# Between the two layers: which products stand ahead of the recurrence, and where z of chunks 1 to 3 is made

## The chip, the cores and the metric

The kernel runs as one program on one core of a Trainium2 chip. The metric is the device time of one execution in microseconds (us). The core has a matrix engine (TensorE, in the profile PE, its weight loads PEld) and three engines for elementwise work: VectorE (DVE), ScalarE (ACT) and GpSimd (POOL). Each takes its own instructions in the order in which they are written and waits on semaphores for the others. SyncE (SP) issues the DMAs here. Operands lie in SBUF; matmuls write PSUM, eight banks of 128 partitions by 512 float32.

## The reference, cut to what matters

Two layers on x of 2048 tokens by 128 features. Layer 0 is an RWKV-like attention with a recurrence and a dense FFN, then a switch FFN with 8 experts. Layer 1 begins with a Mamba block and ends with 16 experts and a shared one. The change lies at the start of the Mamba block:

```python
xz = einsum('bld,ed->ble', x, in_proj_w)            # x here: layernorm(x) * (1 + ca) + sa
xb, zb = xz[..., :256], xz[..., 256:]
u  = silu(causal_conv4(xb) + conv_b)
proj = einsum('bld,ed->ble', u, x_proj_w)           # dt_raw 8, b 16, c 16, a_gate_raw 256
dt = softplus(dt_raw @ dt_proj_w.T + dt_proj_b)
a  = -exp(A_log) * (0.5 + sigmoid(a_gate_raw))
state = exp(dt * a) * state + dt * b_t * u_t        # for 256 channels x 16 states, over 2048 tokens
y_t   = sum(state * c_t) + D_param * u_t
y = y * silu(zb)                                    # zb is first needed here
out = einsum('ble,de->bld', y, out_proj_w)
```

## The kernel before, in words

Features lie on the 128 partitions and tokens along the free axis. The 2048 tokens are cut into four chunks of 512 (`NCH`, index i), the 256 inner channels into two halves (`DI`, index c). Every instruction of this part therefore has the form 128 x 512.

The order on each engine is written out by hand. `sequences()` lists the steps of each engine in order, and each step adds one to its engine's semaphore; `upto(step, i)` is the value that a waiting engine needs. Nothing is reordered at run time: what stands behind a waiting instruction waits too.

**The section between the layers.** For each chunk: the layernorm of layer 1 (`centre_e`, `var_e` on PE, `stats_e` on ACT, `norm_e` on DVE) gives HC; `xb(i)` multiplies HC by the first half of in_proj, `xb_copy` takes it to SBUF, and `conv(c, i)` on DVE adds the taps in PSUM (one scaling, three multiply-adds); `u(i)` on ACT applies Silu. `bc(i)` on PE makes b, c and dt_raw from u; `proj_out(i)` on ACT takes out b, c as bfloat16 (`bc_hi`) and dt_raw (`dt_raw_copy`). `bc_r1` (DVE), `bc_mid` (ACT) and `bc_lo` (POOL) split the rest of b and c into two further bfloat16 parts. `dt(i)` multiplies dt_raw, `softplus(i)` makes the step sizes. `z(i)` multiplies HC by the second half of in_proj and `z_silu(i)` applies Silu to it; that is silu(zb), which `gated(i)` on POOL first needs when a chunk's recurrence is over. `gate0` and `gate1` make a_gate_raw; only chunk 0 has its gates here.

PSUM is shared out by hand: chunk i has the banks i and 4+i (`half(0, i)` and `half(1, i)`), used one after the other by xb, z, bc, the gates and dt. So z(i) waits for u(i), and bc(i) waits for z_silu(i), since they use the same banks.

**The recurrence.** It is 64 turns, q = 16 i + n, for chunk i and state n. PE broadcasts b and c of the state to 128 partitions (`b{n}`, `c{n}`, banks 4 and 5). DVE multiplies b by dt u for both halves (`dbu`, one instruction of 128 x 1024), and runs two scans over the tokens (`st{n}_0`, `st{n}_1`). ACT copies c (`c_copy`) and makes the two decays with Exp (`dec`) in banks 6 and 7. POOL multiplies state by c for each half (`times_c`, `sc{n}_c`), and every second turn copies the last columns for the next chunk (`carry`); this comes behind the step of its turn in `STEP_POOL`. PE adds the products of turn q - 4 (`y_sum`). DVE issues dbu(q+1) ahead of the scans of turn q. The rings couple the engines: the scans of an even turn q wait for the carry of turn q - 3, those of an odd turn for the carry of turn q - 4.

Other work is laid into the turns by tables: `GATE_PE` and `GATE_ACT` (the gates of chunks 1 to 3: products into banks 2 and 3, a Tanh, and an Identity that adds two), `STEP_POOL` (`dtg` and `du`, one POOL multiply each), `SPLIT_AT` (every fourth turn from 18 to 50 ACT rounds and POOL subtracts a block of expert weights, `w_hi`, `w_lo`), `SIDE` (behind a chunk: skip, gated, m_out, x_mamba, the layernorm with `norm_f`, the router) and `GATE_AT` (the router's top-8, small DVE instructions, from turn 34 on). After turn 63 come 68 turns of the experts, on which the change does nothing.

**Lines.** Front: L730 xb and z; L762 bc and gates; L775 dt; L1098 u; L1103 z_silu; L1092 and L1093 proj_out; L1107 bc_mid; L1119 softplus; L1138 and L1145 table loads; L1462 and L1467 conv; L1456 bc_r1; L1268 the last step of norm_e; L1500 dtg of chunk 0; L1662 bc_lo. Recurrence: L908 b and c; L1511 dbu; L1534 scans; L1178 c_copy; L1184 dec; L1111 and L1114 the gates' Tanh and Identity; L1626 every POOL multiply (times_c, dtg, du, gated); L1700 w_lo; L815 y_sum; L1237 skip; L1516 x_mamba; L1520 and L1522 norm_f; L1548 the first step on the router's scores.

Of the kernel before, what the change touches and what calls it, by code (L numbers as in the profile page):

```python
# [58 lines left out]
def side_names(engine, k, i):  # L59
# [11 lines left out]
GATE_PE = {0: [("gate0", 1)], 1: [("gate1", 1)], 2: [("gate0", 2)], 3: [("gate1", 2)],  # L71
           4: [("gate0a", 3)], 5: [("gate0", 3)], 6: [("gate1a", 3)], 7: [("gate1", 3)]}
GATE_ACT = {1: (0, 1), 2: (1, 1), 3: (0, 2), 4: (1, 2), 6: (0, 3), 8: (1, 3)}
STEP_POOL = {4: ("dtg_0", 1), 6: ("dtg_1", 1), 8: ("du_0", 1), 10: ("du_1", 1), 12: ("dtg_0", 2), 14: ("dtg_1", 2), 16: ("du_0", 2), 20: ("du_1", 2),
             24: ("dtg_0", 3), 28: ("dtg_1", 3), 32: ("du_0", 3), 36: ("du_1", 3)}
# [3 lines left out]
       "c0", "c1", "eps5", "eps6", "two",  # L79
# [44 lines left out]
def one(*steps):  # L124
    return [(s, 0) for s in steps]


def sequences():
# [60 lines left out]
    for e in range(E0):  # L189
# [27 lines left out]
    for q in range(NQ + TURNS + LAG_E):  # L217
# [68 lines left out]
def build(nc, X_in, vec_in, core_in, cst_in, wA_in, wmod_in, cstB_in, wB1_in, wB2_in, wC_in, sel_in, eyeb_in, wD_in, out):  # L286
# [17 lines left out]
    with ctx:  # L304
# [142 lines left out]
        HC = area(te_at + T, T)  # L447
# [17 lines left out]
        DRAW = area(place_at[0] + T, T)  # L465
# [73 lines left out]
        def _(pe):  # L539
# [225 lines left out]
            def bc(i):  # L765
                pe.wait_ge(*upto("z0_silu", i))
                x_proj(half(1, i, BC3 + DTR), i, DI * P, BC3 + DTR).then_inc(*done("bc", i))

            def dt(i):
                a = wc_at["dtp"][0]  # L770
                pe.wait_ge(*upto("dt_raw_copy", i))
                for c, w in enumerate((["z1_silu"], ["bc_r1"]) if i else (["gate0_tanh"], ["gate1_tanh"])):
# [8 lines left out]
            z(1)  # L781
# [3 lines left out]
            bc(1)  # L785
            dt(0)
            z(2)
            dt(1)
            bc(2)
            z(3)  # L790
            dt(2)
            bc(3)
            dt(3)

            def gates(q):
                for step, i in GATE_PE.get(q, ()):
                    c = int(step[4])
                    cs = range(DI) if i < NCH - 1 else range(1) if step[-1] == "a" else range(1, DI)
# [124 lines left out]
        def _(act):  # L923
# [196 lines left out]

            xb_copy(2)
# [24 lines left out]
            bc_mid(3)  # L1146
# [673 lines left out]
```

## Time and profile before

| what | us |
|---|---|
| median of 3 runs | 746.44 (746.33 to 746.46) |
| the profiled execution's own time | 746.32 |
| its span, first to last instruction | 744.5 |
| busy: PE / DVE / ACT / POOL | 599.6 / 559.7 / 377.4 / 376.8 |
| mean granted clock of TensorE | 0.912 |
| first scan of the recurrence starts | 324.30 |
| the two scans of the last turn, 63, start | 564.84 |

Times in the profile count from the first instruction. Idle time of an engine costs something only where the chain of waits passes through it. A Matmul in float32 appears as two records. Positions in the recurrence are named by turn: turn q begins where its first scan begins.

### The profile page before, as it was taken

The numbers are of one execution on the slowest core, as the hardware profiler recorded it, in microseconds if no ns is written. First come the engines' busy times: TensorE is split into PE (matmuls) and PEld (weight loads), VectorE is DVE, ScalarE is ACT, GpSimd is POOL, SyncE is SP. The second block draws the span as 40 slices with busy tenths as digits, with TensorE's granted clock in tenths as the row PEclk, the third lists the DMA queues.
The fourth block names the chain that finished last, engine by engine and source line by source line (L and its number), as shares of the span: only waits on it lengthen the run. The fifth ranks groups of instructions, "written<-read, shape, count | busy, mean of one in ns | idle before, by whom it ended". The sixth has DMA issues, their size and how long they took to land.

```text
span 744.5 us, 6787 instructions
## 1 busy us (share of the span) xinstructions
PE 599.6 (81%) x1964; PEld 326.5 (44%) x1964; DVE 559.7 (75%) x771; ACT 377.4 (51%) x657; POOL 376.8 (51%) x330
## 2 busy tenths in 40 slices
PE   6696777589699977878866776677678998999997
PEld 3232222156567732223322232233224666777775
DVE  1757995735767675479999999999996775756564
ACT  4573001696554166677565663456554446544443
POOL 0005666252000110248998986779776544655554
PEclk9698766689799999989999998799999999999999
DMA  8000002400000000100001000000000000000000
GB/s 295 2 2 0 0 1 92 209 1 0 0 1 1 1 0 0 43 0 0 0 5 36 24 22 22 21 11 0 1 0 0 1 1 14 2 0 15 1 15 15
DMA packets 4036, 15.93 MB, mean 21 GB/s; under 512 B 704, under 2 KB 960, under 8 KB 3520
## 3 DMA queue, kind: packets, MB, share of 16 engines
q1 hardware_dynamic: 4000, 15.51, 5.9%
q8 instruction: 16, 0.26, 0.1%
q14 instruction: 20, 0.16, 0.1%
HBM read 14.46 MB, written 1.05 MB: 21 GB/s over the span
## 4 chain that ended last, share of the span: by engine, by line
PE 28%; POOL 22%; DVE 22%; issue 20%; ACT 6%; DMA 1%; POOLq 0%; DVEq 0%; SPq 0%; ACTq 0%
POOL h_parts L1731 11%; POOL arena L1626 10%; DVE arena L1534 9%; PE ps L547 5%; DVE arena L1511 5%; PE ps L815 2%; PE ps L762 2%; PE ps L713 2%; PE ps L675 2%; PE ps L730 1%; PE ps L698 1%; DVE arena L1325 1%; PE ps L615 1%; PE ps L684 1%; PE ps L865 1%
## 5 line engine op out<-in xcount | busy, mean ns | idle before, releaser
L1626 POOL TENSOR_TENSOR arena<-arena 128x512 f32<-128x512 f32 x186 | 229.3, 1257 | 79.8 <-DVE arena L1534 41.2
L1534 DVE TENSOR_TENSOR_SCAN arena<-ps,carry,arena 128x512 f32<-128x512 f32 x128 | 156.3, 1261 | 0.0
L1184 ACT ACTIVATE ps<-arena,abase 128x512 f32<-128x512 f32 x128 | 88.1, 691 | 98.8 <-DVE arena L1534 98.6
L815 PE MATMUL ps<-arena,core 128*128 128x512 f32 x256 | 128.4, 625 | 0.0
L1731 POOL TENSOR_TENSOR h_parts<-arena,h_parts 128x512 fp32r<-128x512 f32 x68 | 88.1, 1297 | 78.8 <-ACT h_parts L1215 78.8
L865 PE MATMUL ps<-x_parts,w_hi 128*128 128x512 f32 x272 | 99.4, 405 | 5.5 <-DVE arena L1615 2.6
L908 PE MATMUL ps<-bc,sel 96*128 96x512 bf16 x128 | 44.3, 406 | 65.4 <-DVE arena L1511 50.5
L1615 DVE TENSOR_TENSOR arena<-ps,arena 128x512 f32<-128x512 f32 x68 | 47.0, 691 | 60.9 <-PE ps L865 52.9
L1223 ACT ACTIVATE arena<-ps 128x512 f32<-128x512 f32 x68 | 40.6, 597 | 88.8 <-PE ps L865 88.8
L1511 DVE TENSOR_TENSOR arena<-ps,arena 128x1024 f32<-128x1024 f32 x64 | 76.7, 1198 | 4.2 <-PE ps L908 4.1
L815 PEld LDWEIGHTS ps<-arena,core 128*128 128x128 f32 x256 | 51.4, 201 | 39.1 <-issue 32.1
L865 PE MATMUL ps<-h_parts,w_hi 128*128 128x512 f32 x136 | 65.8, 486 | 1.2 <-POOL h_parts L1731 1.2
L908 PEld LDWEIGHTS ps<-bc,sel 96*128 96x128 bf16 x128 | 11.5, 99 | 120.1 <-DVE arena L1511 88.4
L865 PEld LDWEIGHTS ps<-x_parts,w_hi 128*128 128x128 f32 x272 | 51.3, 189 | 18.9 <-DVE arena L1615 3.0
L547 PE MATMUL ps<-arena 128*128 128x512 f32 (+2 forms) x80 | 43.3, 692 | 14.1 <-POOL arena L1626 8.5
L865 PE MATMUL ps<-x_parts,wD 128*128 128x512 f32 x136 | 53.7, 395 | 0.0
L929 ACT ACTIVATE arena<-ps 128x512 f32<-128x512 f32 x16 | 9.4, 597 | 79.8 <-PE ps L547 64.1
L1658 POOL TENSOR_TENSOR x<-arena,x 128x512 f32<-128x512 f32 x4 | 5.4, 1342 | 86.9 <-DVE arena L1449 86.9
L1619 DVE TENSOR_TENSOR arena<-ps,arena 128x512 f32<-128x512 f32 x64 | 44.3, 692 | 2.2
L1215 ACT ACTIVATE h_parts<-arena 128x512 fp32r<-128x512 f32 x68 | 42.4, 623 | 0.8 <-DVE arena L1619 0.5
L590 PE MATMUL ps<-v_parts,spread_r 128*128 128x512 f32 x64 | 29.0, 565 | 16.4 <-DVE arena L1325 14.2
L1325 DVE TENSOR_TENSOR_SCAN arena<-arena,ps 128x512 f32<-128x512 f32 x32 | 40.5, 1267 | 0.0
(223 smaller groups left out, 1008.5 us busy)
## 6 DMA issues: line engine op xcount, KB each, us to landing
arena<-in_wB SPq DMA_DIRECT2D x2, 2048.0 KB, 12.6
arena<-in_wD SPq DMA_DIRECT2D x8, 384.0 KB, 3.1
arena<-in_cstB SPq DMA_DIRECT2D x1, 1368.0 KB, 5.9
x<-in_x SPq DMA_DIRECT2D x4, 256.0 KB, 4.9
out_x<-x SPq DMA_DIRECT2D x4, 256.0 KB, 2.0
arena<-in_wA SPq DMA_DIRECT2D x1, 928.0 KB, 9.7
wC<-in_wC SPq DMA_DIRECT2D x1, 912.0 KB, 10.9
arena<-in_wmod SPq DMA_DIRECT2D x1, 768.0 KB, 6.5
```

The lines of the kernel that those rows point to most:

```text
L547: mm(half(h, i, rows), lhsT, ch(rhs, i)[0:parts], start=True, stop=True).then_inc(*done(step, i))
L815: mm(bank(c + 2 * (i % 2)), CORE_("eye"), PRC[:, (2 * q + c) % PR_RING, :], start=(n == 0), stop=(n == NS - 1)).then_inc(*done(f"y{n}_{c}" ...
L865: r = mm(out, w_parts[wp][:, k, :], x[xp], start=start and (wp, xp) == (0, 0), stop=stop and last)
L908: mm(bank(b), sel[:, row, :], BC[:, i * N:(i + 1) * N], start=True, stop=True).then_inc(*done(f"{kind}{n}", i))
L1184: A(bank(6 + c), ch(DTG[:, c, :], i), ACT.Exp, scale=ABASE[:, c * NS + n:c * NS + n + 1]).then_inc(*done(f"dec{n}_{c}", i))
L1325: nc.vector.tensor_tensor_scan(S[:, v, i * N + 1:(i + 1) * N + 1], ch(DEC, i), bank(4 + q % 4), S[:, v, i * N:i * N + 1], ALU.mult, ALU.ad ...
L1511: tt(DBU[:, a:a + DI, :], bank(4).unsqueeze(1).to_broadcast([P, DI, N]), DU[:, :, i * N:(i + 1) * N], ALU.mult).then_inc(*done(f"dbu{n}", i))
L1534: nc.vector.tensor_tensor_scan(ST[:, k % ST_RING, :], bank(6 + c), DBU[:, (2 * q + c) % DBU_RING, :], CARRY[:, k:k + 1], ALU.mult, ALU.add ...
L1615: tt(HH[:, k, :], bank(6), SG[:, k, :], ALU.mult).then_inc(*done(f"hh{e}", i))
L1619: tt(HW[:, k, :], bank(7), HH[:, k, :], ALU.mult).then_inc(*done(f"hw{e}", i))
L1626: mul = lambda o, a, b: nc.gpsimd.tensor_tensor(o, a, b, ALU.mult)
L1731: nc.gpsimd.tensor_tensor(HWP[:, 1, q % 4, :], (HW if e < E1 else HH)[:, q % 2, :], HWP[:, 0, q % 4, :].bitcast(f32), ALU.subtract).then_i ...
```

## The change

- In the section between the layers `z` and `z_silu` are left for chunk 0 alone. `xb(3)` goes ahead of `z(0)`. The order on PE becomes xb 3, z 0, bc 0, gate0, bc 1, gate1, bc 2, dt 0, bc 3, dt 1, dt 2, dt 3; ACT and DVE follow (conv(1, 2) ahead of the first bc_r1, the bc_mid further back). `bc(i)` waits for `u1` in place of `z0_silu`.
- z of chunks 1 to 3 is made in turns 10 to 15 of the recurrence: one product of PE per turn into bank 2 or 3, and on ACT, one turn later, three instructions: tanh(z/2) to ZT, z/2 to Z, and ZT + 1. POOL multiplies the two (`z_full`), six multiplies in turns 12, 14, 15, 16, 25 and 28. The other POOL steps move back by up to eight turns.
- The gates of chunks 1 to 3 start one turn later; gate1 of chunk 2 is split into two half products as those of chunk 3 are.
- HC, the tanh values and dt_raw move to other places in SBUF.

```diff
-GATE_PE = {0: [("gate0", 1)], 1: [("gate1", 1)], 2: [("gate0", 2)], 3: [("gate1", 2)],
-           4: [("gate0a", 3)], 5: [("gate0", 3)], 6: [("gate1a", 3)], 7: [("gate1", 3)]}
-GATE_ACT = {1: (0, 1), 2: (1, 1), 3: (0, 2), 4: (1, 2), 6: (0, 3), 8: (1, 3)}
-STEP_POOL = {4: ("dtg_0", 1), 6: ("dtg_1", 1), 8: ("du_0", 1), 10: ("du_1", 1), 12: ("dtg_0", 2), 14: ("dtg_1", 2), 16: ("du_0", 2), 20: ("du_1", 2),
-             24: ("dtg_0", 3), 28: ("dtg_1", 3), 32: ("du_0", 3), 36: ("du_1", 3)}
+GATE_PE = {1: [("gate0", 1)], 2: [("gate1", 1)], 3: [("gate0", 2)], 4: [("gate1a", 2)], 5: [("gate1", 2)],
+           6: [("gate0a", 3)], 7: [("gate0", 3)], 8: [("gate1a", 3)], 9: [("gate1", 3)],
+           10: [("z0", 2)], 11: [("z1", 2)], 12: [("z0", 3)], 13: [("z1", 3)], 14: [("z0", 1)], 15: [("z1", 1)]}
+GATE_ACT = {2: ("gate", 0, 1), 3: ("gate", 1, 1), 4: ("gate", 0, 2), 6: ("gate", 1, 2), 8: ("gate", 0, 3), 10: ("gate", 1, 3),
+            11: ("z", 0, 2), 12: ("z", 1, 2), 13: ("z", 0, 3), 14: ("z", 1, 3), 15: ("z", 0, 1), 16: ("z", 1, 1)}
+STEP_POOL = {4: ("dtg_0", 1), 6: ("dtg_1", 1), 8: ("du_0", 1), 10: ("du_1", 1), 12: ("z0_full", 2), 14: ("z1_full", 2), 15: ("z0_full", 3), 16: ("z1_full", 3),
+             17: ("dtg_0", 2), 20: ("dtg_1", 2), 21: ("du_0", 2), 24: ("du_1", 2), 25: ("z0_full", 1), 28: ("z1_full", 1),
+             29: ("dtg_0", 3), 32: ("dtg_1", 3), 36: ("du_0", 3), 40: ("du_1", 3)}
...
             def bc(i):
-                pe.wait_ge(*upto("z0_silu", i))
+                pe.wait_ge(*upto("u1", i))
+                if i == 0:
+                    pe.wait_ge(*upto("z0_silu", i))
...
             def gates(q):
                 for step, i in GATE_PE.get(q, ()):
+                    if step[0] == "z":
+                        c = int(step[1])
+                        pe.wait_ge(*upto(f"gate{c}_tanh", NCH - 1))
+                        if i != 2:
+                            pe.wait_ge(*upto(f"z{c}_half", {3: 2, 1: 3}[i]))
+                        a = wc_at["in"][0] + DI * P
+                        mm(bank(2 + c), wC[:, a + c * P:a + (c + 1) * P], ch(HC, i), start=True, stop=True).then_inc(*done(step, i))
+                        continue
...
+            def z_parts(c, i):
+                act.wait_ge(*upto(f"z{c}", i))
+                A(ZT[c, i], bank(2 + c), ACT.Tanh, scale=0.5).then_inc(*done(f"z{c}_tanh", i))
+                A(ch(Z[:, c, :], i), bank(2 + c), ACT.Copy, scale=0.5).then_inc(*done(f"z{c}_half", i))
+                act.wait_ge(*upto(f"z{c}_tanh", i))
+                A(ZT[c, i], ZT[c, i], ACT.Identity, bias=col("one")).then_inc(*done(f"z{c}_one", i))
...
             xb_copy(2)
             u(0)
             xb_copy(3)
             z_silu(0)
             proj_out(0)
+            u(1)
             gate_tanh(0, 0)
-            u(1)
-            bc_mid(0)
-            z_silu(1)
-            gate_tanh(1, 0)
             proj_out(1)
             u(2)
-            z_silu(2)
-            bc_mid(1)
+            gate_tanh(1, 0)
             proj_out(2)
             u(3)
-            z_silu(3)
+            bc_mid(0)
             nc.scalar.preload_act_table_set("softplus")
             softplus(0)
+            proj_out(3)
+            bc_mid(1)
+            softplus(1)
             bc_mid(2)
-            proj_out(3)
-            softplus(1)
+            bc_mid(3)
             softplus(2)
             softplus(3)
             nc.scalar.preload_act_table_set("exp_and_others")
-            bc_mid(3)
...
+            def z_full(c, i):
+                pool.wait_ge(*upto(f"z{c}_one", i))
+                mul(ch(Z[:, c, :], i), ch(Z[:, c, :], i), ZT[c, i]).then_inc(*done(f"z{c}_full", i))
```

## Rows read from the trace of the kernel before

**Rows 1.** Busy time by stretch: us, then each engine, granted clock, DMA, GB/s

```profile
281.00:324.30 43.30, 35.80 (x71) 13.05 (x72) 21.31 (x28) 27.47 (x46) 7.02 (x6) 0.88 0.06 19
...
360.00:380.00 20.00, 13.52 (x35) 5.28 (x34) 20.00 (x18) 11.02 (x18) 18.06 (x17) 1.00 0.00 0
```

**Rows 2.** Chain of waits, 304 to 326: start us, us, what

```profile
305.91 3.34 PE ps L730 x4
...
314.62 3.58 ACT arena L1119 x6
...
319.28 3.41 PE ps L762 x4
```

**Rows 3.** Timeline before turn 0: start, us, engine line, xcount, [idle before <-who ended it]

```profile
277.88 0.55 DVE L1268 TENSOR_SCALAR arena<-arena,mod 128x512 f32<-128x512 f32 x1
280.18 1.09 ACT L1098 ACTIVATE arena<-ps 128x512 f32<-128x512 f32 x2
281.43 4.58 DVE L1467 SCALAR_TENSOR_TENSOR ps<-arena,vec,ps 128x512 f32<-128x512 f32 x6
288.01 0.59 ACT L1092 ACTIVATE bc<-ps 96x512 bf16<-96x512 f32 x1 [1.57 <-PE ps L762]
290.87 1.98 PE L730 MATMUL ps<-arena,wC 128*128 128x512 f32 x4 [1.18 <-ACT arena L1098]
309.91 1.28 ACT L1138 ACT_TABLE_LOAD   x1
318.89 1.22 DVE L1511 TENSOR_TENSOR arena<-ps,arena 128x1024 f32<-128x1024 f32 x1 [1.10 <-PE ps L908]
323.16 1.22 DVE L1511 TENSOR_TENSOR arena<-ps,arena 128x1024 f32<-128x1024 f32 x1 [3.04 <-PE ps L908]
324.30 2.45 DVE L1534 TENSOR_TENSOR_SCAN arena<-ps,carry,arena 128x512 f32<-128x512 f32 x2
```

**Rows 4.** Timeline of turns 3 and 4, PE and ACT

```profile
333.34 0.60 PE L908 MATMUL ps<-bc,sel 96*128 96x512 bf16 x2
335.14 0.72 ACT L1114 ACTIVATE arena<-arena,vec 128x512 f32<-128x512 f32 x1
335.50 1.02 PE L762 MATMUL ps<-arena,wC 128*128 128x512 f32 x2
336.35 0.60 PE L908 MATMUL ps<-bc,sel 96*128 96x512 bf16 x2
```

**Rows 5.** Groups of POOL, 326 to 563: busy us, mean ns

```profile
L1626 POOL TENSOR_TENSOR arena<-arena 128x512 f32<-128x512 f32 x142 | 176.5, 1272 | 42.3 <-DVE arena L1534 40.3 <-ACT arena L1178 1.0 <-PE ps L908 0.9
L1700 POOL TENSOR_TENSOR wD<-arena,w_hi 128x768 fp32r<-128x768 f32 x8 | 14.5, 1812 | 1.8 <-ACT w_hi L1189 1.7
```

**Rows 6.** Timeline of turns 12, 28 and 34, DVE, then POOL

```profile
366.24 2.44 DVE L1534 TENSOR_TENSOR_SCAN arena<-ps,carry,arena 128x512 f32<-128x512 f32 x2
...
423.91 2.44 DVE L1534 TENSOR_TENSOR_SCAN arena<-ps,carry,arena 128x512 f32<-128x512 f32 x2
427.02 1.02 DVE L1522 TENSOR_SCALAR arena<-arena,mod 128x512 f32<-128x512 f32 x1
429.10 2.44 DVE L1534 TENSOR_TENSOR_SCAN arena<-ps,carry,arena 128x512 f32<-128x512 f32 x2
446.50 2.44 DVE L1534 TENSOR_TENSOR_SCAN arena<-ps,carry,arena 128x512 f32<-128x512 f32 x2
449.08 3.47 DVE L1548 TENSOR_SCALAR arena<-arena 128x64 f32<-128x64 f32 x1
454.13 2.45 DVE L1534 TENSOR_TENSOR_SCAN arena<-ps,carry,arena 128x512 f32<-128x512 f32 x2
...
425.26 3.91 POOL L1626 TENSOR_TENSOR arena<-arena 128x512 f32<-128x512 f32 x3
448.25 1.80 POOL L1700 TENSOR_TENSOR wD<-arena,w_hi 128x768 fp32r<-128x768 f32 x1
450.02 2.47 POOL L1626 TENSOR_TENSOR arena<-arena 128x512 f32<-128x512 f32 x2
```

More of the change, by code:

```diff
@@ L78 @@
 VEC = ["ln1_w", "mu_r", "mu_k", "mu_v", "mu_w", "mu_g", "w0", "u", "gn_w", "gn_b", "ln2_w",
-       "c0", "c1", "eps5", "eps6", "two",
+       "c0", "c1", "eps5", "eps6", "two", "one",
        "dt_b0", "dt_b1", "D0", "D1", "cb0", "cb1"] + [f"cw{c}_{j}" for c in range(DI) for j in range(KC)] + \
@@ L446, in build @@
         TE = area(te_at, T)
[L447 removed]
+        HC = over_arena("layer_in", WD_AT + 2 * T, T, f32)
+        tanh_at = [te_at + (2 + c) * N for c in range(DI)] + [WD_AT + E0 * 2 * P + k * N for k in range(4)]
+        assert tanh_at[-1] + N <= WD_AT + 2 * T
+        ZT = {(c, i): over_arena(f"z_tanh{c}_{i}", tanh_at[2 * (i - 1) + c], N, f32) for i in range(1, NCH) for c in range(DI)}
         XBP = area(xbp_at, DI * (T + 3)).rearrange("p (c t) -> p c t", c=DI)
@@ L771, in dt @@
                 pe.wait_ge(*upto("dt_raw_copy", i))
-                for c, w in enumerate((["z1_silu"], ["bc_r1"]) if i else (["gate0_tanh"], ["gate1_tanh"])):
+                for c, w in enumerate(([], ["bc_r1"]) if i else (["gate0_tanh"], ["gate1_tanh"])):
                     for name in w:
@@ L784, in _ @@
             x_proj(half(1, 0), 0, P, P).then_inc(*done("gate1", 0))
-            bc(1)
+            bc(2)
             dt(0)
-            z(2)
+            bc(3)
             dt(1)
-            bc(2)
-            z(3)
             dt(2)
-            bc(3)
             dt(3)
+            halves = [item for items in GATE_PE.values() for item in items if item[0][-1] == "a"]
             def gates(q):
                 for step, i in GATE_PE.get(q, ()):
+                    if step[0] == "z":
[6 more added lines that the diff above has]
+                        continue
                     c = int(step[4])
-                    cs = range(DI) if i < NCH - 1 else range(1) if step[-1] == "a" else range(1, DI)
+                    split = (f"gate{c}a", i) in halves
+                    cs = range(DI) if not split else range(1) if step[-1] == "a" else range(1, DI)
                     if 0 in cs and i > 1:
@@ L1486, in _ @@
             conv(0, 2)
+            conv(1, 2)
             bc_r1(0)
-            conv(1, 2)
-            bc_r1(1)
             conv(0, 3)
@@ L1495, in _ @@
             nc.vector.memset(CARRY[:], 0.0).then_inc(*done("st_zero"))
+            bc_r1(1)
             bc_r1(2)
@@ L1749 @@
     vecs = dict(L0, u=L0["u"].reshape(-1), gn_w=by_value(L0["gn_w"].reshape(-1), 0), gn_b=by_value(L0["gn_b"].reshape(-1), 0),
-                c0=a["L0_c"][0], c1=a["L1_c"][0], eps5=np.full(P, 1e-5, np.float32), eps6=np.full(P, 1e-6, np.float32), two=np.full(P, 2, np.float32))
+                c0=a["L0_c"][0], c1=a["L1_c"][0], eps5=np.full(P, 1e-5, np.float32), eps6=np.full(P, 1e-6, np.float32), two=np.full(P, 2, np.float32), one=np.full(P, 1, np.float32))
     x = np.ascontiguousarray(L0["x"][0].T)
```

40 lines of the change are left out of this document (22 added, 18 removed).

## Prediction

> **What bounds the kernel now.** I read the busy time by stretch first. Between the layers, 281 to 324.3, no engine is full: PE 35.8 of 43.3 us, ACT 27.5, DVE 21.3, and the granted clock is 0.88 [rows 1]. That is a stretch of waits. In the recurrence DVE is busy 20.00 of 20 us, PE, ACT and POOL 13.5, 11.0 and 18.1 [rows 1]: there DVE sets the pace, and POOL is the next by far.
>
> The chain of waits says which waits end last in the first stretch: the product z(3) (3.34 us, at the lower clock), the softplus run on ACT, and, behind the start of the recurrence, a gate product of 3.41 us [rows 2]. z of chunks 1 to 3 is in that chain although nobody needs it before a chunk's recurrence is over. The timeline gives the start of the recurrence [rows 3]: the last softplus ends at 318.20 (314.62 + 3.58 [rows 2]), dbu(0) starts at 318.89, dbu(1) only at 323.16, after 3.04 us without work on DVE, and the first scan at 324.30. From there DVE runs on to the experts, so what moves the first scan moves the end, if the turns keep their length.
>
> **The section between the layers.** It loses three z (six products) and six Silu, and with them the waits of bc(i) for z_silu. I follow the new order with the durations of [rows 3]: a product over both halves 1.91 apart from the next (four records, 1.98), a pair of u or z_silu 1.09, proj_out 2 x 0.62, a table 1.28, a conv of three 2.3 (4.58 for six) and 0.85 more where its scaling is on DVE; softplus 0.60 each (3.58 / 6 [rows 2]).
> - xb(3) need not wait for u(0) any more: modE(3) ends at 278.43 (277.88 + 0.55), the product at 280.4. u(0) ends at 281.27 as before, xb_copy(3) at 282.9, z(0) on PE at 282.7, z_silu(0) at 284.0, its first half at 283.5.
> - bc(0) 283.55 to 285.5, gate0 to 287.3; ACT proj_out(0) to 286.8, u(1) to 287.9; bc(1) to 289.85.
> - ACT Tanh, proj_out(1) to 291.1, u(2) to 292.2 (its conv runs through, from 286.01 = 281.43 + 4.58 to 289.15); bc(2) to 294.2, dt(0) to 296.1.
> - Conv of chunk 3 ends at 295.15 on DVE (bc_r1(0) 0.7, then 2.3 and 3.15). ACT: proj_out(2) to 295.4, u(3) to 296.55, bc_mid(0) to 297.15, table to 298.4, softplus(0) to 299.65, proj_out(3) to 300.9 (bc(3) 296.6 to 298.5).
> - From here ACT has work without a gap: bc_mid(1), softplus(1), bc_mid(2) and (3), softplus(2) and (3): 3 x 0.62 + 6 x 0.60 = 5.5, to 306.4. PE has dt(1), dt(2), dt(3) done at 300.4, 302.3, 304.3, ahead of need.
>
> So the last softplus ends at 306.4, before 318.2: **11.8 us**. ACT's removed Silus are only 3.3 of it; the rest are waits.
>
> **The start of the recurrence.** With no gate in turn 0, b(1) goes out when dbu(0) has ended. dbu(0) starts 0.65 behind the softplus (0.69 before), takes 1.22, b(1) about 0.5, dbu(1) 1.14 until the scan: 3.6 us, before 324.30 - 318.20 = 6.1. ACT covers it: table 1.28, c_copy 0.5, first decay 0.7 are over after 2.5. **2.5 us**. First scan at 310.0; 14.3 us in sum. POOL's du(0) waits only for bc_mid(0) and softplus(0) and is over by 302. If the clock is at 1.2 GHz in the three dt products, each takes up to 3.34 in place of 1.98 and ACT would wait some 3 us; if the reordered waits are all free, ACT's idle 4 us are the floor. I keep 11 to 16 for this part.
>
> **PE and ACT in the turns.** PE with a half gate takes 3.01 us from b to b (333.34 to 336.35) of a turn of 3.48; a z product takes the same 1.02 as a half gate [rows 4], in turns 10 to 15, so it hides. ACT is busy 11.02 of 20 us without gates, 1.92 a turn [rows 1]; z adds three instructions of at most 0.72 [rows 4], 1.8 to 2.2: 3.7 to 4.1, or about 3.5 when each begins some 0.1 before the last one's record ends (the records overlap so). A turn is 3.48. The decay ends about 0.9 us ahead of its scan, which covers six turns of a slip of 0.1; at 0.6 a turn the six would cost 2.7. I take zero, of 0 to 2.7. The gates one turn later cost nothing, since dtg(1) on POOL stays in turn 4. The expert weights' first DMAs hang on the last conv on SP's queue and go out 8 us earlier, into a stretch whose other work needs no DMA; the later ones wait for w_lo, up to 3 us late, for a split four turns (14 us) on: nothing.
>
> **POOL.** Six multiplies of 1.24 us (pitch; 1272 ns mean duration [rows 5]) are new: 7.4 us. A turn of POOL is 2.49 and 0.14 for a carry every second turn; it can start its first multiply 1.35 behind the first scan (425.26 - 423.91 [rows 6]), so a turn leaves it 0.9 idle; a step costs 1.24 and a split 1.77, more than the idle time. From turn 12 to turn 28 DVE needs 423.91 - 366.24 = 57.7 us [rows 6]. POOL's work in these 16 turns: 39.8 for the states, 1.1 carries, 5.3 for the splits of 18, 22 and 26, 2.5 gated of turn 21, and nine steps, before five: 11.2, before 6.2. In sum 59.9, and about 2 of waits at the start. It ends turn 27 at 61.9 of the new time, where turn 28's first multiply could start at 59.0: **2.9 us behind**. In before it is not behind there (it starts at exactly 1.35). By the same count it ends turn 34 at 88.2 where 84.1 would be on time, 4.1 behind; the most is 4.8 in turn 22.
>
> Being behind is free while the waits allow it. The scans of turn 30 need the carry of 27 (61.9 against 66.3), those of 34 that of 31 (76.4 against 80.25); PE adds the products only four turns later, so it bears some 7 us. So no scan waits for POOL.
>
> What is not free are DVE instructions that both read and write SBUF. modF of turn 28 lasts 1.02 and had begun while POOL multiplied; the router's first, 128 x 64 only, lasts 3.47 [rows 6]: it begins at 449.08, and ends at 452.55, just when POOL's run (w_lo to 450.05, two multiplies to 452.49) is over. DVE got in between two POOL instructions in the first case (427.75), and at the end of the run in the second. So:
> - low end: DVE gets in at the next boundary in turn 28 (62.0, +0.2 against before), and waits for the run's end in turn 34: 88.5 (88.2 and the 0.3 that POOL lost to modF), that is 8.1 behind the turn's begin, where before it was 6.05 (452.55 - 446.50). **2.3 us lost.** The wait lets POOL catch up, so it is paid once; turns 36 and 40 have one step each as 32 and 36 had, with POOL on time.
> - high end: it waits for the run's end in turn 28 too, to 65.9 in place of 61.8: 4.1; then turn 34 costs 0.5 more than before: **4.6 us lost**.
> - below: in turn 34 it gets in early, and 2 of the 3.4 us that before loses come back.
> I take 2.3, as each of the two waits goes as it did before.
>
> The Trainium skill (SBUF — State Buffer, Who interferes with whom) says that a DVE instruction in a two-port mode, or with two SBUF inputs, and a GpSimd instruction exclude each other, and that the second to issue is blocked until the first finishes. By this rule the cost is one POOL instruction at most, and the change would be better by 4 us than my sum; the 3.47 us, across three POOL instructions, disagree.
>
> **Sum.** 746.32 - 14.3 + 2.3 = 734.3 for an execution like the profiled one; the median is 0.12 above it. I predict **734.4**.
>
> **Rivals.**
> - *POOL is paid for in full.* Each of DVE's SBUF instructions waits for the run's end, or scans wait for the carry: 4.6 to 7.4 in place of 2.3. For: POOL 18.06 of 20 us, the 3.47. Against: the low end of the count above. 737 to 739.5; I give 738.
> - *One POOL instruction at most*, the page's rule, worked out here: in turn 34 the request at 83.0 meets the multiply that ends at 84.1, so the router's first step is over 2.3 us earlier against the turn than before, and +0.2 remains in turn 28. 746.4 - 14.3 - 2.1 = 730. For: 427.75. Against: 449.08.
> - *The front gives less.* Another wait is last, such as conv of chunk 3 or dt at 1.2 GHz; the last softplus at 311: 739.
> - *Slower.* PE falls to 1.2 GHz in turns 4 to 15: its turn of 3.01 becomes 6, as z(3) took 3.34 where z(1) took 1.98 [rows 2, 3]. Each such turn costs 2.5, and from the sixth on (2.5 x 6 > 14.3) the kernel is slower; 12 turns give 762. For: 0.88 ahead of the recurrence. Against: PE has more to do in these turns than before, and the clock was 1.00 in the later stretch with less work [rows 1].
> - That the change does not do what it says (some z back in the chain) I count with the third.
>
> **Chances.** Forecast 0.60, POOL in full 0.15, one instruction 0.12, front less 0.09, slower 0.03; 0.01 for no change. Within 0.2% (1.5 us) is what a measurement of this kernel can't tell from none. The forecast's own range is 732.5 to 736.5; with the first and second rival I give 730 to 739, which leaves the rest out. Faster 0.96, same 0.01, slower 0.03.
>
> **What would show it.** First scan near 310 and last softplus near 306.4; no DVE gap between dbu(0) and dbu(1) beyond b(1)'s 0.6; turns of 3.48 up to 19; POOL without idle time from 14 to 34; modF of turn 28 1.0 to 1.3 us (4 or more: the high end); the router's first step of turn 34 about 5.5 us. A turn above 4 between 1 and 19 would prove me wrong on PE or ACT, an idle DVE ahead of a scan on POOL's carry. The stretch from the last scan to the end should stay as it is.

## The result, and the profile after

| what | before | changed |
|---|---|---|
| median of four runs, us | 746.45 (746.33 to 754.95) | 736.14 (736.06 to 736.99) |
| ratio of the means, 95% interval | | 0.9838 (0.9802 to 0.9874) |
| the profiled execution's own time / span | 746.32 / 744.5 | 736.99 / 735.0 |
| mean granted clock | 0.912 | 0.913 |

The kernel became 10.3 us faster; 734.4 was forecast, with 730 to 739 as the range. The ratio of the medians is 0.986; that of the means is lower because one run of before took 754.95. In the later batches of this study before has medians of 746.65, 748.39, 748.33 and 748.94, and the changed kernel, run again beside the second of them, 736.44; the ratio given with each run below is against before in its own batch. Both profiled executions fall into the same pieces:

| stretch, us | before | changed | difference | forecast |
|---|---|---|---|---|
| start to the last layernorm step's end | 278.43 | 279.41 | +1.0 | 0 |
| to the end of the last softplus | 39.77 | 27.58 | -12.2 | -11.8 |
| to the first scan | 6.11 | 3.77 | -2.3 | -2.5 |
| turns 0 to 19 | 69.78 | 70.57 | +0.8 | 0 |
| turns 20 to 27 | 29.82 | 29.82 | 0 | 0 |
| turns 28 to 33 | 22.60 | 22.37 | -0.2 | +0.2 |
| turns 34 to 38 | 29.17 | 30.76 | +1.6 | +2.1 |
| turns 39 to 62 | 89.17 | 88.52 | -0.7 | 0 |
| end of the last scan (turn 63) to the end | 177.26 | 179.73 | +2.5 | 0 |

Turn 63's two scans, 2.43 us in both, lie between the last two rows. The first piece is not touched by the change: over the profiles of this study its last step starts between 276.8 and 279.7. The rest I take from the rows that follow.

The timeline before turn 0 in the changed kernel (start, us, engine and line; it answers to [rows 3]):

```profile
278.86 0.55 DVE L1289 TENSOR_SCALAR layer_in<-layer_in,mod 128x512 f32<-128x512 f32 x1
...
304.60 2.39 ACT L1135 ACTIVATE arena<-ps,vec 128x512 f32<-128x512 f32 x4
...
307.69 1.23 DVE L1532 TENSOR_TENSOR arena<-ps,arena 128x1024 f32<-128x1024 f32 x1 [4.66 <-PE ps L924]
...
309.62 1.22 DVE L1532 TENSOR_TENSOR arena<-ps,arena 128x1024 f32<-128x1024 f32 x1 [0.70 <-PE ps L924]
...
309.80 3.62 PE L768 MATMUL ps<-arena,wC 128*128 128x512 f32 x4
...
310.76 2.45 DVE L1555 TENSOR_TENSOR_SCAN arena<-ps,carry,arena 128x512 f32<-128x512 f32 x2
...
313.21 1.06 PE L924 MATMUL ps<-bc,sel 96*128 96x512 bf16 x2
...
313.88 1.22 DVE L1532 TENSOR_TENSOR arena<-ps,arena 128x1024 f32<-128x1024 f32 x1 [0.68 <-PE ps L924]
315.03 2.45 DVE L1555 TENSOR_TENSOR_SCAN arena<-ps,carry,arena 128x512 f32<-128x512 f32 x2
```

The last softplus ends at 306.99, where before it ended at 318.20; DVE now waits 0.70 us for b(1), before 3.04. But the gate product, 3.62 us long, now stands ahead of b(2): b(2) and c(2) run from 313.21 to 314.27, dbu(2) can start only at 313.88 with b(2) done, DVE waits 0.68, and turn 0 is 4.27 us (310.76 to 315.03) in place of 3.48.

The chain of waits of the same stretch (start, us, what; it answers to [rows 2]):

```profile
298.08 1.28 ACT L1157
...
299.38 1.26 ACT arena L1135 x2
300.64 0.48 ACT bc L1108
...
303.67 1.03 ACT bc L1123 x2
304.70 2.30 ACT arena L1135 x4
```

From the table load at 298.08 to the end at 306.99 ACT is busy 8.82 of 8.91 us: what ends last here is ACT's own work and no longer a product of PE. The windows, as [rows 1], with the expert stretch of both kernels and 8 us out of it (before's at 620, the changed kernel's at 608, each 55 us behind turn 63):

```profile
281.96:310.76 28.80, 24.27 (x50) 8.33 (x51) 19.13 (x28) 23.64 (x40) 8.49 (x6) 0.88 0.09 28
346.52:366.52 20.00, 17.32 (x44) 6.74 (x45) 20.00 (x19) 18.95 (x35) 18.07 (x18) 1.00 0.00 0
552.79:732.00 179.21, 173.89 (x717) 123.80 (x717) 109.91 (x215) 84.42 (x148) 97.13 (x77) 0.97 0.02 5
608.00:616.00 8.00, 5.42 (x22) 3.87 (x21) 3.81 (x6) 4.17 (x7) 2.85 (x2) 0.79 0.00 0
```

Before:

```profile
564.84:742.00 177.16, 171.38 (x717) 122.33 (x717) 110.34 (x215) 84.42 (x148) 97.10 (x77) 0.99 0.02 5
620.00:628.00 8.00, 5.94 (x29) 4.37 (x30) 5.17 (x8) 4.64 (x10) 3.81 (x3) 1.00 0.00 0
```

The expert stretch has the same instructions in both (717, 215, 148, 77) and takes 2.5 us more in the changed kernel's profile, at a mean clock of 0.97 against 0.99; one of the places is the window at 608, granted 0.79.

Turns 28 and 34 in the changed kernel, DVE and then POOL (they answer to [rows 6]):

```profile
411.15 2.45 DVE L1555 TENSOR_TENSOR_SCAN arena<-ps,carry,arena 128x512 f32<-128x512 f32 x2
...
414.27 0.79 DVE L1543 TENSOR_SCALAR arena<-arena,mod 128x512 f32<-128x512 f32 x1
...
433.52 2.44 DVE L1555 TENSOR_TENSOR_SCAN arena<-ps,carry,arena 128x512 f32<-128x512 f32 x2
...
436.09 5.06 DVE L1569 TENSOR_SCALAR arena<-arena 128x64 f32<-128x64 f32 x1
...
442.74 2.44 DVE L1555 TENSOR_TENSOR_SCAN arena<-ps,carry,arena 128x512 f32<-128x512 f32 x2
...
409.81 4.96 POOL L1647 TENSOR_TENSOR arena<-arena 128x512 f32<-128x512 f32 x4
...
430.61 6.17 POOL L1647 TENSOR_TENSOR arena<-arena 128x512 f32<-128x512 f32 x5
...
436.71 0.20 POOL L1732 COPY carry<-arena 128x4 f32<-128x4 f32 x1
436.85 1.81 POOL L1725 TENSOR_TENSOR wD<-arena,w_hi 128x768 fp32r<-128x768 f32 x1
438.61 2.49 POOL L1647 TENSOR_TENSOR arena<-arena 128x512 f32<-128x512 f32 x2
```

The router's first step (+1 on a 128 x 64 tile in SBUF) starts at 436.09, while POOL multiplies, and ends at 441.15, 0.05 behind the end of POOL's run at 441.10. In both kernels the step starts 2.6 us behind the turn's begin. POOL's run ends 7.58 behind it in the changed kernel and 5.99 in before, since POOL is behind: the step takes 5.06 us in place of 3.47. Turn 34 is 9.22 us, before 7.63.

### The profile page after: what moved, and what is told of

It reads as the page before. It is cut to its first block, busy times and chain, and to the rows that moved or that the text cites. A ratio compares the mean times of both kernels' runs of the same rounds, so it can differ in the third digit from the quotient of the medians.

```text
span 735.0 us, 6807 instructions
## 1 busy us (share of the span) xinstructions
PE 598.5 (81%) x1964; PEld 327.0 (44%) x1964; DVE 558.8 (76%) x771; ACT 382.4 (52%) x669; POOL 385.5 (52%) x336
## 4 chain that ended last, share of the span: by engine, by line
POOL 29%; PE 24%; issue 21%; DVE 18%; ACT 7%; DMA 1%; POOLq 0%; DVEq 0%; SPq 0%; ACTq 0%
POOL arena L1647 17%; POOL h_parts L1759 11%; DVE arena L1555 6%; PE ps L553 5%; DVE arena L1532 3%; PE ps L719 2%; PE ps L831 2%; PE ps L681 2%; PE ps L768 2%; PE ps L704 1%; DVE arena L1346 1%; PE ps L621 1%; DVE ps L1488 1%; PE ps L881 1%; PE ps L690 1%
```

## Experiments

Three questions: where the gain at the front comes from, what POOL's six multiplies cost, and whether a better version follows.

**1. z of chunks 1 to 3 left out of the changed kernel.**

```diff
-           10: [("z0", 2)], 11: [("z1", 2)], 12: [("z0", 3)], 13: [("z1", 3)], 14: [("z0", 1)], 15: [("z1", 1)]}
+           }
...
-            11: ("z", 0, 2), 12: ("z", 1, 2), 13: ("z", 0, 3), 14: ("z", 1, 3), 15: ("z", 0, 1), 16: ("z", 1, 1)}
+            }
...
-12: ("z0_full", 2), 14: ("z1_full", 2), 15: ("z0_full", 3), 16: ("z1_full", 3), ... 25: ("z0_full", 1), 28: ("z1_full", 1),
...
-                    mul(ch(U[:, c, :], i), ch(U[:, c, :], i), ch(Z[:, c, :], i)).then_inc(*done(f"gated_{c}", i))
+                    mul(ch(U[:, c, :], i), ch(U[:, c, :], i), ch(U[:, c, :], i)).then_inc(*done(f"gated_{c}", i))
```

> The changed kernel with the z of chunks 1 to 3 left out wholly: no product, no tanh, no z/2, no +1, no POOL multiply (gated multiplies u by itself there). Theory: what z costs in the recurrence is POOL's lag alone, paid in turn 34, where the router's first DVE step waited 5.06 us against 3.47 before. So that step is back at about 3.5, modF of turn 28 at 1.0, the turns of 10 to 17 stay at 3.48, and the time is 734.7 (736.1 - 1.6 + 0.2). Rival: PE or ACT pay too, then more than 2 us are gained and some turn of 10 to 17 was longer than 3.48.

Measured: median 733.36, ratio 0.984 (0.9785 to 0.9896), the runs from 732.27 to 741.64. The profiled execution is that of 741.64, and its front took 32.67 us from the last layernorm step to the last softplus, 5.1 more than the changed kernel's, with the same instructions. The three dt products and the window there:

```profile
300.00:316.00 16.00, 14.33 (x19) 4.69 (x19) 4.97 (x5) 11.49 (x19) 6.26 (x6) 0.50 0.03 10
```

```profile
301.56 10.60 PE L781 MATMUL ps<-arena,wC 8*128 8x512 f32 x12
```

In the changed kernel the same twelve records are

```profile
299.50 6.28 PE L783 MATMUL ps<-arena,wC 8*128 8x512 f32 x12
...
299.00:306.50 7.50, 6.79 (x14) 2.27 (x12) 1.89 (x3) 7.41 (x14) 6.65 (x6) 0.83 0.06 25
```

So the front has a long form, with the clock at 1.2 GHz (0.50 granted) from bc(3) through the dt products: the third rival's 1.2 GHz, real but only in some executions. Behind the front, turns 0 to 19 took 70.52 as in the changed kernel: z's products and ACT's three instructions cost the turns nothing. The other three runs, 732.27 to 733.73, have no trace; the median is 2.8 below the changed kernel's, and 1.3 below the 734.7 expected. More than 2 us are gained, as the rival had it, but no turn from 10 to 17 of the changed kernel is longer than 3.48, so PE and ACT are not shown to be the source. The turns from 20 to 38 give little of that: turn 28 took 5.88 (4.96 with z), turn 34 7.95 (9.22); their pieces sum to 82.16 against 82.95. modF of turn 28 was not back at 1.0: it took 1.71 us, to 421.83, where POOL's run ended at 421.55.

**2. Only the six multiplies left out.**

```diff
-12: ("z0_full", 2), 14: ("z1_full", 2), 15: ("z0_full", 3), 16: ("z1_full", 3), ... 25: ("z0_full", 1), 28: ("z1_full", 1),
```

> The changed kernel without POOL's six z multiplies (chunks 1 to 3 are gated by z/2); PE and ACT still make z/2 and 1 + tanh. Theory (only POOL's lag costs): the same time as with z left out wholly, 734.7, within 0.3. Rival (PE or ACT pay): it stays near 736.1 and above the run with z left out.

Measured: 735.86, ratio 0.9849 (0.9831 to 0.9866). Turns 20 to 38 take 29.82 + 23.73 + 29.50 = 83.05 us, with the multiplies 29.82 + 22.37 + 30.76 = 82.95. **Six multiplies fewer on POOL gain nothing there**, and the median, 735.86, is 0.3 below the changed kernel's, where 734.7 was expected. Turn 34 gives back what was forecast (7.95; the router's step 3.80), but turn 28 takes it: 6.32 against 4.96. DVE and POOL in turn 28:

```profile
412.28 2.15 DVE L1543 TENSOR_SCALAR arena<-arena,mod 128x512 f32<-128x512 f32 x1
```

```profile
411.65 2.49 POOL L1647 TENSOR_TENSOR arena<-arena 128x512 f32<-128x512 f32 x2
```

Here modF, 0.79 us in the changed kernel, waits for both multiplies (to 414.14) and ends at 414.43. In the changed kernel it asked at 414.27, shortly before a multiply ended (414.77), and got in there. Here it met a boundary too (412.92), and did not get in. The cost hangs on where POOL's run stands when DVE asks, not on how far POOL is behind.

**3. Before, with z of chunks 1 to 3 left out and the old order kept.**

```diff
-            z(1)
...
             dt(0)
-            z(2)
             dt(1)
             bc(2)
-            z(3)
             dt(2)
...
-                pe.wait_ge(*upto("z0_silu", i))
+                pe.wait_ge(*(upto("u1", i) if i else upto("z0_silu", i)))
```

> The kernel before with z and its Silu of chunks 1 to 3 left out, everything else in its old order and the gates in turn 0 (gated multiplies u by itself there). Theory: z was in the chain, so its products, Silus and the waits on them are most of the 14.5 us by which the first scan came earlier: followed with the old order, the last softplus ends at about 309.5 in place of 318.2, the first scan starts 6 behind it as before, near 315.5, and the time is 737.7. Rival: the new order of convolutions, bc and dt is what counts, z was mostly beside other waits; then the softplus ends after 314 and the time is 742 or more.

Measured: 741.19, ratio 0.9935 (0.991 to 0.9959). In the profile the last softplus comes 36.42 us behind the layernorm step, before 39.77 and in the changed kernel 27.58. Taking z out of the old order brings 3.4 of the 12.2 us in this execution. The medians differ by 5.3 (of 10.3), but that isn't the front alone: of the 7.4 us of the two profiled spans 2.9 come from turns 34 to 38, see below. I had put its softplus at 309.5; it ended at 314.76. PE shows why it is later:

```profile
297.54 3.74 PE L762 MATMUL ps<-arena,wC 128*104 128x512 f32 x4
302.58 3.78 PE L775 MATMUL ps<-arena,wC 8*128 8x512 f32 x4 [1.30 <-ACT arena L1090]
306.28 3.63 PE L762 MATMUL ps<-arena,wC 128*104 128x512 f32 x4
```

bc(2), dt(2) and bc(3), all three in the chain that ended last, run at 0.50 to 0.55 granted (297.5 to 310), 3.6 to 3.8 us each where z(1) took 1.98 [rows 3]. That is 5.2 us more (an estimate from these rows), nearly the 5.3 by which the softplus is late. So two readings stand side by side: with the clock that PE was granted here, z brings 3.4 us and the new order 8.8; had these three products taken 1.98, z would bring up to 8.6 and the order 3.6 or more. No run has the old order without z at full clock, so the share of each is not shown. And this run holds the plainest case of the router's step. POOL's work around turn 34 has the timing of before to 0.01 us of the turn's begin, and yet:

```profile
443.08 2.44 DVE L1528 TENSOR_TENSOR_SCAN arena<-ps,carry,arena 128x512 f32<-128x512 f32 x2
...
445.66 1.04 DVE L1542 TENSOR_SCALAR arena<-arena 128x64 f32<-128x64 f32 x1
```

```profile
444.83 1.81 POOL L1694 TENSOR_TENSOR wD<-arena,w_hi 128x768 fp32r<-128x768 f32 x1
446.60 2.50 POOL L1620 TENSOR_TENSOR arena<-arena 128x512 f32<-128x512 f32 x2
```

The step ends at 446.70, at the boundary behind `w_lo` (446.64): 1.04 us, where before waited through the two multiplies as well, 3.47 [rows 6]. Turn 34 is 5.20 instead of 7.63.

**4. The router's + 1 on ACT for chunks 0 to 2.**

```diff
-                    ts(scores(i, 1), scores(i, 0), 1.0, None, ALU.add).then_inc(*done("g_one", i))
-                    dve.wait_ge(*upto("g_one", i))
+                    dve.wait_ge(*upto("g_plus", i))
...
+                    act.wait_ge(*upto("g_act", i))
+                    A(scores(i, 1), scores(i, 0), ACT.Identity, bias=col("one")).then_inc(*done("g_plus", i))
```

> The changed kernel with the router's first step for chunks 0 to 2, a 128 x 64 tensor_scalar that adds one, on ACT in place of DVE. Theory: DVE's wait of 5 us in turn 34 was for SBUF access while POOL ran without a pause, by that form of instruction; without it turn 34 takes about 4.3 us in place of 9.2, POOL keeps its lag of 4 us, the later small steps of turns 35 to 38 may wait one or two us more, and the time is 732 to 733.5. Rival 1: the wait passes to the reciprocal or the next two-input step, then 735.5 to 736. Rival 2: with the lag kept the scans wait for POOL's carry, seen as idle DVE ahead of a scan, and half of the gain is gone.

Measured: 737.6 (734.89 to 738.8), ratio 0.9868 (0.984 to 0.9896), where 732 to 733.5 was expected; the profiled one, 738.77, had the long front (32.65), 5.1 us more than the changed kernel's. The step left DVE, turn 34 fell to 4.06 us, and turn 35 rose to 7.55:

```profile
441.50 0.49 DVE L1572 RECIPROCAL arena<-arena 128x64 f32<-128x64 f32 x1
...
445.35 3.71 DVE L1578 TENSOR_TENSOR arena<-arena,wC 128x64 f32<-128x64 f32 x1
```

```profile
444.04 4.94 POOL L1648 TENSOR_TENSOR arena<-arena 128x512 f32<-128x512 f32 x4
```

The next instruction of DVE with two operands in SBUF took over the wait: it ends at 449.06, POOL's run at 448.98. The reciprocal, with one operand, went through beside POOL in 0.49 us; the + 1 and modF, with one operand too, had waited in the runs above. Turns 34 to 38 are 28.99 us, 1.8 below the changed kernel's: the first rival, that the wait passes to the next step with two inputs, is what the trace shows.

**5. The changed kernel once more**, to see what differs from one execution to the next.

> The changed kernel itself, once more. In two variants of it the stretch from the last layernorm step to the last softplus took 32.7 us in place of 27.6, with TensorE granted 0.5 from bc(3) through the dt products. Theory: this is a property of the new front in some executions, not of those edits; then some of the runs here are 3 to 6 us above 736.1, and where the profile shows 0.5 in that stretch the last softplus is 5 us late. Rival: all runs within 0.5 us of 736.1, and the edits caused it.

Measured: 736.44, ratio 0.9847 (0.9827 to 0.9867). Every piece of the table behind the first repeats within 0.06 us (27.59, 3.77, 70.57, 29.83, 22.38, 30.79, 88.53, 179.79), the router's step with 5.08 us too. So the waits between DVE and POOL and the expert stretch of 179.7 come again in a second execution. The long front did not show in any of the eight runs of the changed kernel: 736.05 to 737.19.

**6. The gates from turn 0 on, as before.**

```diff
-GATE_PE = {1: [("gate0", 1)], 2: [("gate1", 1)], 3: [("gate0", 2)], 4: [("gate1a", 2)], 5: [("gate1", 2)],
+GATE_PE = {0: [("gate0", 1)], 1: [("gate1", 1)], 2: [("gate0", 2)], 3: [("gate1", 2)],
...
-GATE_ACT = {2: ("gate", 0, 1), 3: ("gate", 1, 1), 4: ("gate", 0, 2), 6: ("gate", 1, 2),
+GATE_ACT = {1: ("gate", 0, 1), 2: ("gate", 1, 1), 3: ("gate", 0, 2), 5: ("gate", 1, 2),
...
```

> The changed kernel with the gates of chunk 1 in turns 0 and 1 again, those of chunk 2 in 2 and 3, the rest as changed. Theory: gate0 stands ahead of b(1) again, so the second dbu is late by the 3 us seen before (first scan 6.1 behind the softplus in place of 3.8), and turn 0 loses the 0.8 that it has with a gate ahead of b(2): 2.35 - 0.8 = 1.5 us slower, 737.6. Rival (as my prediction had it, turn 0 costs nothing): 2.4 slower, 738.5.

Measured: 736.42, ratio 0.985 (0.9826 to 0.9874). DVE before turn 0:

```profile
306.44 1.22 DVE L1532 TENSOR_TENSOR arena<-ps,arena 128x1024 f32<-128x1024 f32 x1 [4.66 <-PE ps L924]
310.20 1.22 DVE L1532 TENSOR_TENSOR arena<-ps,arena 128x1024 f32<-128x1024 f32 x1 [2.54 <-PE ps L924]
```

The wait for b(1) is 2.54 in place of 0.70, and the first scan comes 5.60 us behind the softplus in place of 3.77: the move of the gates by one turn is worth 1.8 us at the start. It saves nothing of the long turn, which becomes turn 1 (4.44) in place of turn 0 (4.27). The median does not show these 1.8 us. In the profiled execution a short expert stretch (177.28 in place of 179.73) hides them; the other three runs have no trace.

**7. The gates by halves, from turn 1 on.**

```diff
+GATE_PE = {1: [("gate0a", 1)], 2: [("gate0", 1)], 3: [("gate1", 1)], 4: [("gate0a", 2)], 5: [("gate0", 2)], 6: [("gate1a", 2)], 7: [("gate1", 2)],
+           8: [("gate0a", 3)], 9: [("gate0", 3)], 10: [("gate1a", 3)], 11: [("gate1", 3)], 12: [("z0", 2)], ... 17: [("z1", 1)]}
...
```

> The changed kernel with the chunk 1 gate0 product as two halves in turns 1 and 2, gate1 in turn 3, and everything behind it up to two turns later. Theory: a half product at the lower clock is 1.7 us, ahead of b(2) it no longer delays dbu(2) much: turn 0 falls from 4.27 to 3.5, turn 2 from 3.64 to 3.5: 0.9 us faster, 735.2. Rival: z later in the turns makes POOL's lag larger in turn 28 and loses it again.

Measured: 736.09, ratio 0.9841 (0.9816 to 0.9867). Turns 0 to 19 take 69.62 us in place of 70.57, and turn 0 is 3.48:

```profile
311.22 2.45 DVE L1555 TENSOR_TENSOR_SCAN arena<-ps,carry,arena 128x512 f32<-128x512 f32 x2
...
314.70 2.45 DVE L1555 TENSOR_TENSOR_SCAN arena<-ps,carry,arena 128x512 f32<-128x512 f32 x2
```

A whole gate product at 1.2 GHz ahead of b(2) was what made turn 0 long. The gain of 1 us is below what the medians tell apart.

**8. dt as a product over 104 rows in place of 8.**

```diff
+                pe.wait_ge(*upto("bc_r1", i))
...
-wC[BC3:BC3 + DTR, a + c * P:a + (c + 1) * P], ch(DRAW, i)[BC3:BC3 + DTR],
+wC[0:BC3 + DTR, a + c * P:a + (c + 1) * P], ch(DRAW, i)[0:BC3 + DTR],
```

> The changed kernel with the dt products over 104 partitions in place of 8: the 96 more rows of the weight are zero, the values added are zero, the number of columns and passes is the same. Theory: TensorE's clock falls in the dt products when it falls at all because they keep only 8 rows of the array busy; with 104 the front has its short form in all runs and the spread between runs shrinks, median at or below 736.1. Rival: the clock depends on something else; the same share of runs has the long form.

```profile
299.00:306.50 7.50, 5.20 (x13) 1.98 (x11) 1.89 (x3) 7.41 (x14) 6.88 (x5) 1.00 0.01 3
```

Measured: 736.82, ratio 0.9859 (0.9832 to 0.9886); at or below 736.1 was expected. In the same window the clock is 1.00 where the changed kernel has 0.83 (mean over the span 0.923 against 0.913), but the last softplus comes 27.61 us behind, as with 8 rows: ACT ends last there, so PE's 0.83 cost nothing. No run of this kernel (up to 738.68) or of the changed one (eight, up to 737.19) stands 5 us above its others, so whether the 104 rows prevent the long front stays open.

**9. The old order of convolutions and bc_r1 on DVE.**

```diff
             conv(0, 2)
-            conv(1, 2)
             bc_r1(0)
+            conv(1, 2)
+            bc_r1(1)
             conv(0, 3)
```

> The changed kernel with DVE's convolutions interrupted again as before (bc_r1(0) ahead of conv(1, 2), bc_r1(1) ahead of conv(0, 3)). Theory: bc_r1(0) waits for bc(0), which ends 0.3 behind the conv of chunk 2, and bc_r1(1) for bc(1): the conv of chunk 3 ends some 1.5 to 2.5 us later, u(3), bc(3) and the softplus with it; last softplus 1.5 to 2.5 later than the changed kernel's 27.6 behind the last layernorm step, time near 738. Rival: the chain goes through ACT and dt, and the conv has slack: the same within 0.3.

Measured: 740.43, ratio 0.9887 (0.9831 to 0.9943), four runs between 735.82 and 744.37. In its profile (its own time 735.82) the last softplus is at 28.27, 0.7 later than with conv(1, 2) ahead, where 1.5 to 2.5 was expected:

```profile
290.32 0.69 DVE L1477 TENSOR_TENSOR arena<-ps,bc 96x512 f32<-96x512 f32 x1 [0.58 <-ACT bc L1108]
```

bc_r1(1) makes DVE wait 0.58 for proj_out(1) and takes 0.69 itself, ahead of conv(0, 3). The runs at 743.94 and 744.37 have no trace. They stand 7.0 to 8.6 us above the other two, more than the 5.1 of the long front; what they are is not shown.

**10. Splits moved away from the router's steps.**

```diff
-SPLIT_AT = {18 + 4 * k: k for k in range(WD_PARTS)}
+SPLIT_AT = {q: k for k, q in enumerate((18, 22, 26, 30, 36, 40, 45, 49, 53))}
```

> The changed kernel with the expert weight splits of turns 34, 38, 42, 46 and 50 put to turns 36, 40, 45, 49 and 53, so that no 1.8 us split stands in POOL's run where the router's small DVE steps come (turns 34 to 38). Theory (DVE's step waits until POOL's unbroken run ends): the step of turn 34 waits 5.06 - 1.77 = 3.3 us, turn 34 takes 7.4 in place of 9.2, and turn 38 5.5 in place of 7.0; 3 us faster, 733.1. Rival (it waits for one POOL instruction at a time, by chance): turn 34 changes by other amounts, between 4.5 and 9.2.

Measured: **732.65**, ratio 0.9794 (0.9746 to 0.9842), 733.1 expected. Five splits have moved, two of them out of turns 34 and 38. Turn 34 is 7.44 us and turn 38 5.51 (7.01 in both kernels). The step and POOL's run:

```profile
434.90 3.29 DVE L1569 TENSOR_SCALAR arena<-arena 128x64 f32<-128x64 f32 x1
```

```profile
435.50 0.20 POOL L1732 COPY carry<-arena 128x4 f32<-128x4 f32 x1
435.65 2.49 POOL L1647 TENSOR_TENSOR arena<-arena 128x512 f32<-128x512 f32 x2
```

The step again ends (438.19) where the run ends (438.14), and the run is shorter by w_lo's 1.8 us. This size was forecast from the theory of the run's end, and came.

**11 and 12. Splits with halves, and all three edits (4, 7 and 10).**

> The splits moved, and the gates of chunk 1 by halves from turn 1. Theory: the two gains add, 3 + 0.9: 732.2. Rival: one of them is taken back by POOL's lag in turns 28 to 34.

> The splits moved, the gates by halves, and the router's +1 on ACT. Theory: in turn 34 no DVE instruction of the blocked forms is left but the reciprocal, which did not wait; the two-input add of turn 35 then waits for the end of POOL's run, 1.8 us less than the 3.7 it waited with a split in the run. Turns 34 and 35 together take about 9.5 in place of 7.1 + 4.2, 1.8 us less: 729.3. Rival: POOL, whose lag is never drained by a DVE stall, makes a later step or scan wait as much: 731.

Measured: 731.03, ratio 0.9784 (0.9741 to 0.9827), and **730.77**, ratio 0.9753 (0.9717 to 0.979), the best here: 5.4 us below the changed kernel's first median, 15.7 below before's 746.45 and 18.2 below before's 748.94 in its own batch. For the last one 729.3 was expected, its rival 731. Its turns 34 and 35:

```profile
432.61 2.44 DVE L1557 TENSOR_TENSOR_SCAN arena<-ps,carry,arena 128x512 f32<-128x512 f32 x2
...
435.18 0.49 DVE L1572 RECIPROCAL arena<-arena 128x64 f32<-128x64 f32 x1
...
439.03 0.33 DVE L1578 TENSOR_TENSOR arena<-arena,wC 128x64 f32<-128x64 f32 x1
```

The two-operand add that waited 3.71 us in run 4 takes 0.33, though POOL multiplies at that moment too (438.01 to 440.51, the boundary at 439.28). Turns 34 to 38 fall to 24.11 us (30.76 in the changed kernel), while turns 28 to 33 rise from 22.37 to 23.56. Against run 11 turns 20 to 38 are 2.2 us shorter in the traces, but the medians differ by 0.3 only: the trace of run 12 has the long expert stretch, that of run 11 the short one.

## Why the prediction was right, and where its sum was not

**The last softplus, 11.8 us: right.** Measured from the last layernorm step the forecast was 27.97 (306.4 - 278.43), and it came at 27.58. The working rested on ACT being without a gap from the table load on, and the chain of waits shows just that. How it divides between the removed z and the new order stays open: in the old order the removal brings 3.4 of 12.2 at the clock that run 3 was granted, and up to 8.6 at full clock, by the estimate given there. The convolution order alone is 0.7 of it, where I had expected more. The full clock was a condition of this forecast that I priced at some 3 us and not more: where it failed, in runs 1 and 4, the same front took 5.1 us longer, and no run shows what makes the clock hold.

**The start of the recurrence, 2.5 us: right** (2.3; run 6, with the gates where they were, gives back 1.8 of it).

**"The gates one turn later cost nothing": wrong, by 0.8 us.** I looked at dtg on POOL, which needs the gate, and not at what the gate product stands ahead of on PE's queue. In turn 0 there is no slack yet, and the clock is at 1.2 GHz (0.50 granted from 309.8 to 313.4): the product takes 3.62 us, and DVE waits 0.68 for b(2). My own half-gate row of 1.02 us [rows 4] came from turns at full clock. Run 7 removes it.

**PE and ACT beside z: right.** Turns 0 to 19 are the same with and without z (70.57, 70.52). The window 346:366 shows what was used up: ACT is at 18.95 of 20 us, where it had 11.02 without [rows 1], and DVE still at 20.00.

**POOL, 2.3 us: the places right, the size and the class of instructions not.** The two places were the right ones: turn 28 forecast at +0.2 and measured -0.2, turn 34 at +2.1 and measured +1.6, the step 5.5 against 5.06. To that come -0.7 in turn 40, where in before x_mamba (L1516) waited 0.58 for PE; its length changes where the edit lies elsewhere (4.17 in the changed kernel, 4.96 in run 6, 5.60 in run 9), so this is not POOL's. In sum 0.7 in place of 2.3. What was wrong is the picture behind it, in which lag on POOL is turned into a cost: run 2 takes the multiplies away and the turns stay as long. And "DVE instructions that both read and write SBUF" is too wide: the scans do that as well, with one operand in PSUM, and take 2.44 us for two beside POOL as without it. Those that waited have all their operands in SBUF, and even of these the reciprocal did not wait (run 4). "POOL is paid for in full" falls with this. "One POOL instruction at most" falls for the changed kernel (5.06 across the end of one multiply, a carry, w_lo and two more multiplies), though run 3 shows a step that did get in at a boundary.

The Trainium skill (SBUF — State Buffer, Who interferes with whom) says that whichever of the two issues first has the shared ports for its whole instruction, and that the other is blocked outright meanwhile. The traces agree that one waits outright: 3.29 us in run 10, 3.71 in run 4, 5.06 here, for steps whose shortest instances in the changed kernel took 0.13 (the + 1) and 0.22 (the add). They agree too that one SBUF operand outside a two-port mode is free (the reciprocal, 0.49). They do not agree that it ends with the instruction that was running: here it mostly ended with POOL's run.

**"The stretch from the last scan to the end should stay as it is": wrong, by 2.5 us.** This is the largest single miss of the sum, and it lies in code that the change does not edit. Over all profiles that stretch is either 176.7 to 177.5 (before, runs 3, 4, 6, 7, 9 and 11) or 179.5 to 179.9 (changed, runs 1, 2, 5, 8, 10 and 12), by how long PE is granted 0.50 at its beginning and again near 55 us into it: the first 6 us behind the last scan have 0.80 to 0.85 granted in the short form and 0.59 to 0.64 in the long one, the stretch from 56 to 60 us behind it 1.00 and 0.57 to 0.63. Whether the change has a part in it is not shown: both traces with the old front are short, both of the changed kernel are long, and its variants are either.

**The sum.** Forecast -12.0 for the profiled execution, measured -9.5 of span: +1.0 upstream, -0.2 front, +0.8 turn 0, -1.6 POOL, +2.5 experts. The 734.4 came within 1.7 of the median in part by luck: the forecast loss on POOL, 1.6 too large, stood against +0.8, +1.0 and +2.5 that it had at nothing. The front's 14.3 us, measured 14.5, are not luck.

**Open.** Where the 2.8 us of run 1's median come from. What decides who gets in at a boundary between two POOL instructions: run 3 and before have the same POOL timing and differ by 2.4 us. What decides between the two forms of the front (27.6 or 32.7) and between the two of the expert stretch: the granted clock shows them, no edit here sets them at will. How much of the front is z and how much the order (run 3). The new places of HC, the tanh values and dt_raw in SBUF were not run by themselves.

## What to carry to other kernels

When work is taken out of a section of waits, follow the new order instruction by instruction to the engine that ends last; the removed Silus are 3.3 us of ACT, and the last softplus came 12.2 us earlier. When work is put on an engine that shares SBUF with the one that sets the pace, don't price it by its length or by its lag: list the pace-setter's instructions with all operands in SBUF and ask what run of the other they will meet; moving splits out of the two turns where they met brought 3.3 us in turns 34 to 38, taking six multiplies out brought none. And look at what stands behind a moved product on its own queue, in the first turn above all.

## What the runs showed of the hardware that was not expected

- A VectorE step on 128 x 64 elements took up to 5.08 us beside GpSimd, through several of its instructions one after another, and the two executions of the changed kernel agree to 0.02 us. With GpSimd's work placed alike to 0.01 us, it took 3.47 us in one kernel and 1.04 in another.
- With fewer products TensorE was busy as long as with more: from 278.4 to 314.7 before's 57 records kept it busy for 27.99 us at 0.95 granted, and without z 48 records did for 28.36 us at 0.79 (run 3, one trace each). The new front itself took 27.6 or 32.7 us with the same instructions and another granted clock.
- The expert stretch, with the same 717 matmuls, took 177 or 180 us, a difference as large as what most edits of this study bring: an edit of 1 to 2 us shows in its own turns and not in the median.
